# A GRU and an RK4 oscillator in one recurrence: order of the new h, the stage bases and the candidate, and 1 - z scaled by ScalarE

## What is computed

```python
def cell(h, x):                                   # layer 0: GRU
    gi = x @ W_ih + b_ih; gh = h @ W_hh + b_hh
    r = sigmoid(i_r + h_r); z = sigmoid(i_z + h_z)
    n = tanh(i_n + r * h_n)
    return (1.0 - z) * n + z * h
def derivative(q, p, drive):                      # layer 1: four of these per step (RK4)
    dq = q - q**3 / 3.0 - p + drive + tanh(q) @ coupling.T + bias
    dp = EPSILON * (q + ALPHA - BETA * p)
```

## Time and profile before

| | us |
|---|---|
| median of 3 runs (lowest, highest) | 3659.93 (3659.13, 3660.63) |
| the profiled execution, its own time | 3661.45 |
| its span | 3659.7 |
| TensorE busy: matmul, weight load | 3546.2, 3220.4 |
| VectorE, ScalarE, GpSimd busy | 2998.4, 2574.2, 1507.0 |

### The profile page before, as it was taken

The page is one execution under the profiler, slowest core; times in us unless marked ns, Lnnn a source line. Parts: engine busy times, 40 slices in busy tenths (PEclk is TensorE's granted clock), DMA queues, the critical chain, the costliest instruction groups (busy, mean ns, idle before and its releaser), DMA issues.

```text
span 3659.7 us, 298613 instructions
## 1 busy us (share of the span) xinstructions
PE 3546.2 (97%) x115469; PEld 3220.4 (88%) x115469; DVE 2998.4 (82%) x20699; ACT 2574.2 (70%) x22689; POOL 1507.0 (41%) x6169
## 2 busy tenths in 40 slices
PE   8989999999999999999999999999999999999978
PEld 4479999999999999999999999999999999999954
DVE  2078888888888888888888888888888888888876
ACT  3257777777777777777777777777777777777753
POOL 0034444444444444444444444444444444444421
PEclk9999999999999999999999999999999999999978
DMA  3000000000000000000000000000000000000001
GB/s 127 23 25 1 1 1 1 1 1 1 1 1 1 1 1 1 1 1 1 1 1 1 1 1 1 1 1 1 1 1 1 1 1 1 1 1 1 1 2 46
DMA packets 9454, 24.45 MB, mean 7 GB/s; under 512 B 557, under 2 KB 601, under 8 KB 8793
## 3 DMA queue, kind: packets, MB, share of 16 engines
q1 hardware_dynamic: 8832, 19.92, 1.5%
q10 hardware_dynamic: 88, 0.02, 0.0%
HBM read 15.75 MB, written 4.19 MB: 5 GB/s over the span
## 4 chain that ended last, share of the span: by engine, by line
PE 79%; DVE 14%; issue 4%; ACT 3%; DVEq 0%; DMA 0%; ACTq 0%; POOL 0%; POOLq 0%
PE psum L1180 43%; PE psum L1138 29%; PE psum L1108 5%; DVE psum L887 2%; DVE tpart L843 2%; DVE gates L776 2%; ACT tpart L571 1%; PE psum L1283 1%; DVE psum L878 1%; DVE psum L866 1%; DVE fresh L795 1%; DVE narg L787 1%; DVE hs L812 1%; ACT tfull L573 1%; DVE hpart L819 0%
## 5 line engine op out<-in xcount | busy, mean ns | idle before, releaser
L1180 PE MATMUL psum<-tpart,cpl 128*128 128x32 f16 x65536 | 1995.8, 177 | 34.1 <-DVE tpart L843 15.0
L1180 PEld LDWEIGHTS psum<-tpart,cpl 128*128 128x128 f16 x65536 | 1788.7, 96 | 150.9 <-DVE tpart L843 41.5
L1138 PE MATMUL psum<-hpart,whh 128*128 128x32 f16 x49152 | 1622.9, 176 | 28.8 <-DVE hpart L819 24.4
L1138 PEld LDWEIGHTS psum<-hpart,whh 128*128 128x128 f16 x49152 | 1404.1, 96 | 91.5 <-DVE hpart L819 30.4
L843 DVE SCALAR_TENSOR_TENSOR tpart<-tfull,tpart 128x8 f16<-128x8 f32 x4096 | 668.4, 163 | 146.6 <-ACT tfull L573 9.9
L571 ACT ACTIVATE tpart<-psum 128x8 f16<-128x8 f32 x3072 | 544.0, 177 | 245.8 <-DVE psum L887 177.2
L887 DVE TENSOR_REDUCE psum<-psum 128x8 f32<-128x24 f32 x3072 | 585.5, 192 | 133.9 <-PE psum L1180 12.2
L573 ACT ACTIVATE tfull<-psum 128x8 f32<-128x8 f32 x3072 | 529.2, 172 | 0.0
L571 ACT ACTIVATE tpart<-qnext 128x8 f16<-128x8 f32 x1024 | 213.9, 209 | 434.6 <-DVE qnext L887 434.5
L535 ACT ACTIVATE qterm<-psum 128x16 f32<-128x16 f32 x3072 | 400.6, 184 | 111.0 <-DVE psum L866 109.1
L374 POOL TENSOR_TENSOR kept<-rz,hs 128x8 f32<-128x8 f32 x1024 | 209.2, 204 | 466.5 <-ACT rz L500 465.6
(11 more groups left out here) (152 smaller groups left out, 4040.5 us busy)
## 6 DMA issues: line engine op xcount, KB each, us to landing
xrow<-in_x_dram SPq DMA_DIRECT2D x4, 1024.0 KB, 11.3
out_dram<-space SPq DMA_DIRECT2D x16, 256.0 KB, 2.0
wih<-in_L_cond_W_ih_dram SPq DMA_DIRECT2D x3, 1024.0 KB, 9.6
space<-in_L_cond_W_hh_dram SPq DMA_DIRECT2D x1, 3072.0 KB, 18.6
space<-in_L_cond_coupling_dram SPq DMA_DIRECT2D x1, 1024.0 KB, 19.2
xrow<-in_cond_dram SPq DMA_DIRECT2D x1, 1024.0 KB, 4.7
wih<-in_L_cond_Wk_dram SPq DMA_DIRECT2D x1, 1024.0 KB, 5.6
wih<-in_L_cond_Wo_dram SPq DMA_DIRECT2D x1, 1024.0 KB, 8.0
```

Source lines behind the costliest of these rows:

```text
L1138: mm = pe.matmul(gate_out[x][:, :, :, c * B:(c + 1) * B], whh[:, w, k, n * P:(n + 1) * P], copies_in(hpart[:, k, :, :]), start=(c == 0 and ...
L1180: mm = pe.matmul(stage_out[a][:, :, :, col:col + B], cpl[:, w, k, n * P:(n + 1) * P], copies_in(tpart[:, s % 2, k, :, :]), start=(col == 0 ...
```

## The change

VectorE: in stage 2 `base(2)` goes ahead of `sum_gates(1)`; in stage 3 the order becomes `cubic(3)`, `weigh(1)`, `base(3)`, `new_high(1)`, `new_h_full(1)`, `h_low(1)`, and only then `sum_stage(3, 0)` and `sum_stage(3, 1)`. `weigh` multiplies two tensors instead of two tensors and a scalar, since ScalarE now scales `omz` into a new tile `omzs` (`scaled_omz`); the first half's runs behind the terms of stage 0, the second half's between the two halves' tanh of stage 2. `split_tanh` subtracts instead of multiplying by 1.0 and subtracting. ScalarE: in stage 2 the square that feeds `cubic(3)` goes ahead of `candidate(1)`. GpSimd: `keep_part(1)` goes behind the sums of stage 2 instead of stage 1.

```diff
--- before.py
+++ after.py
@@ -116,6 +116,7 @@
         gates = sb("gates", [P, HALVES, HG])
         rz = sb("rz", [P, HALVES, 2 * HC])
         omz = sb("omz", [P, HALVES, HC])
+        omzs = sb("omzs", [P, HALVES, HC])
         gated = sb("gated", [P, HALVES, HC])
         narg = sb("narg", [P, HALVES, HC])
         cand = sb("cand", [P, HALVES, HC])
@@ -255,6 +256,7 @@
 
         h_parts, gibase_ready, ka_read, h_ready = sem_ab("h_parts"), sem("gibase_ready"), sem("ka_read"), sem("h_ready")
         gate_mm, gate_sum, rz_ready, omz_ready = sem_ab("gate_mm"), sem_ab("gate_sum"), sem_ab("rz_ready"), sem_ab("omz_ready")
+        omzs_ready = sem_ab("omzs_ready")
         gated_ready, narg_ready, cand_ready = sem_ab("gated_ready"), sem_ab("narg_ready"), sem_ab("cand_ready")
         kept_ready, fresh_ready, hi_ready, hs_ready = sem_ab("kept_ready"), sem_ab("fresh_ready"), sem_ab("hi_ready"), sem_ab("hs_ready")
 
@@ -406,7 +408,7 @@
                     if s == 1 and tail <= T:
                         next_x1(tail, now)
                         next_uhat(tail)
-                    if s == 1 and gru <= T:
+                    if s == 2 and gru <= T:
                         keep_part(1, gru)
 
                 if tail <= T:
@@ -480,6 +482,8 @@
                 act.reg_load(r, kap[0:1, n:n + 1].bitcast(i32))
             k_unh = act.alloc_register("act_scale_h")
             act.reg_load(k_unh, inv[0:1, 0:1].bitcast(i32))
+            k_h = act.alloc_register("act_scale_up")
+            act.reg_load(k_h, scale[0:1, 2:3].bitcast(i32))
             k_minus = act.alloc_register("act_scale_minus")
             act.reg_load(k_minus, kap[0:1, 5:6].bitcast(i32))
             k_c = act.alloc_register("act_scale_c")
@@ -500,6 +504,11 @@
                 act.activation(rz[:, x, :], gates[:, x, HC:HG], ACT.Sigmoid, scale=k_gate).then_inc(rz_ready[x], 1)
                 act.activation(omz[:, x, :], gates[:, x, 2 * HC:HG], ACT.Sigmoid, scale=k_minus).then_inc(omz_ready[x], 1)
 
+            def scaled_omz(x, v):
+
+                act.wait_ge(omz_ready[x], v)
+                act.activation(omzs[:, x, :], omz[:, x, :], ACT.Copy, scale=k_h).then_inc(omzs_ready[x], 1)
+
             def candidate(x, v):
 
                 act.wait_ge(narg_ready[x], v)
@@ -517,6 +526,8 @@
                 gate_input(v)
                 sigmoids(0, v)
                 sigmoids(1, v)
+                scaled_omz(0, v)
+                scaled_omz(1, v)
                 candidate(0, v)
                 candidate(1, v)
                 plain_h(v)
@@ -574,10 +585,10 @@
                                        scale=k_stage[s]).then_inc(tanh_ready[s][a], 1)
                         if s == 1 and a == 0 and gru <= T:
                             candidate(0, gru)
+                        if s == 2 and a == 0 and gru <= T:
+                            scaled_omz(1, gru)
                     if s == 2:
                         stage_terms(2)
-                        if gru <= T:
-                            candidate(1, gru)
                     arg, s_next = (in_halves(qnext[:, :]), 0) if s == 3 else (qt, s + 1)
                     if s < 3 or tail <= T:
                         act.activation(in_halves(sq[:, s_next, :]), arg, ACT.Square,
@@ -589,6 +600,8 @@
                             sigmoids(0, gru)
                         act.wait_ge(cub_ready, stage_count(1, now))
                         stage_terms(0)
+                        if gru <= T:
+                            scaled_omz(0, gru)
                         if 3 <= tail <= T:
                             plain_h(tail)
                     if s == 1:
@@ -598,6 +611,8 @@
                         stage_terms(1)
                         if gru <= T:
                             sigmoids(1, gru)
+                    if s == 2 and gru <= T:
+                        candidate(1, gru)
                     if s == 2 and gru < T:
                         gate_input(gru + 1)
                     if s == 3 and tail <= T:
@@ -790,10 +805,9 @@
 
             def weigh(x, v):
 
-                dve.wait_ge(omz_ready[x], v)
+                dve.wait_ge(omzs_ready[x], v)
                 dve.wait_ge(cand_ready[x], v)
-                dve.scalar_tensor_tensor(fresh[:, x, :], omz[:, x, :], s_h, cand[:, x, :],
-                                         ALU.mult, ALU.mult).then_inc(fresh_ready[x], 1)
+                dve.tensor_tensor(fresh[:, x, :], omzs[:, x, :], cand[:, x, :], ALU.mult).then_inc(fresh_ready[x], 1)
 
             def new_high(x, v):
 
@@ -840,9 +854,9 @@
             def split_tanh(s, a, v, ready, n):
 
                 dve.wait_ge(ready, n)
-                dve.scalar_tensor_tensor(tpart[:, s % 2, a * HK:(a + 1) * HK, 1, :],
-                                         tfull[:, a * HC:(a + 1) * HC].rearrange("p (k b) -> p k b", b=B), 1.0,
-                                         tpart[:, s % 2, a * HK:(a + 1) * HK, 0, :], ALU.mult, ALU.subtract).then_inc(t_parts[s][a], 1)
+                dve.tensor_tensor(tpart[:, s % 2, a * HK:(a + 1) * HK, 1, :],
+                                  tfull[:, a * HC:(a + 1) * HC].rearrange("p (k b) -> p k b", b=B),
+                                  tpart[:, s % 2, a * HK:(a + 1) * HK, 0, :], ALU.subtract).then_inc(t_parts[s][a], 1)
 
             for a in range(HALVES):
                 split_tanh(0, a, 1, tanh0_ready, a + 1)
@@ -932,8 +946,9 @@
                 if gated_step:
                     new_high(0, gru)
                     new_h_full(0, gru)
+                base(2, now)
+                if gated_step:
                     sum_gates(1, gru)
-                base(2, now)
                 if gru < T:
                     h_low(0, gru)
 
@@ -945,18 +960,17 @@
                     argument(1, gru)
                 split_tanh(3, 0, now, tanh_ready[2][0], now)
                 split_tanh(3, 1, now, tanh_ready[2][1], now)
+                cubic(3, now)
                 if gated_step:
                     weigh(1, gru)
-                cubic(3, now)
+                base(3, now)
                 if gated_step:
                     new_high(1, gru)
-                base(3, now)
-                if gated_step:
                     new_h_full(1, gru)
-
-                sum_stage(3, 0, now)
                 if gru < T:
                     h_low(1, gru)
+
+                sum_stage(3, 0, now)
                 sum_stage(3, 1, now)
                 if tail <= T:
                     split_tanh(0, 0, tail, tanh_ready[3][0], now)
```

## The result

The changed kernel takes 3710.12 us (median of 4 runs, 3707.46 to 3713.26), the kernel before in the same rounds 3660.23. The ratio is 1.0137, 95% interval 1.012 to 1.0155: 49.9 us slower. The forecast was 3731, in a range of 3696 to 3757. The granted clock was 0.989 over the span, as before. Ratios in this document leave out executions in a second, slower state of the chip; e5's slowest run is one.

A forecast was written before the change was run, and what follows sets the result against it. TensorE was nearly always busy, its next stage 0 released by two level chains. A reduce 0.17 later cost 0.16 per step, less 0.02 for the loop turn: 0.14 x 510 = 71 us, median 3731, range 3696 to 3757.

The forecast's parts named there:

- The bound: TensorE's next stage 0 waits for two level releasers, `h_low(1)` and `split_tanh(0, 0)`; shortening only one gains nothing.
- Part 3, the place of the reduce: VectorE, stage 3: the first reduce, now behind `h_low(1)`, starts 0.17 later; stage 0 follows, 0.16 us per step.
- Part 1, the first half: Stage 2, first half of h: `weigh(0)` 0.08 shorter, but `sum_gates(1)` 0.05 later; stage 3 starts 0.04 later.
- Part 2, the candidate: ScalarE, stage 3: `candidate(1)` behind the square comes 0.12 later, 0.05 inherited and 0.07 from the square; `weigh(1)` 6.00, was 5.88.
- Part 1, `scaled_omz`: Two more ScalarE activations fit into free queue time and cost nothing; upper bound 0.10 of delay.
- The turn of the loop: TensorE's loop turn may hide in its new wait, giving back 0 to 0.04 per step; half taken.
- A: Rival, faster: both releasers of stage 0 come earlier, needing `new_high(1)` before 6.07; 0.10 per step, 3609; chance 0.08.
- B: Rival, slower still: `scaled_omz(1)` delays the second tanh pair by 0.10; 0.24 per step, 3782; chance 0.05.
- C: Rival, no change: waits on the own engine cost no queue time, reduce at 6.55; 3660; chance 0.07.
- D: Rival, better cover: loop turn goes wholly, half the stalls fall into new gaps; 0.07 per step, 3696; chance 0.12.
- The rule weighed: Skill's rule that chained semaphores cost nothing extra would make VectorE's order nearly free; rows showed 0.17 of queue time against it.

The follow-up runs named there:

- e5: The kernel before with four steps instead of two in the body of TensorE's loop: 3793.88 us, ratio 1.034 without the slowest run.
- e1: The changed kernel with `h_low(1)` back between the two reduces of stage 3: 3604.47 us, 0.9847 of the kernel before.
- e2: The kernel before with only `h_low(1)` moved ahead of `sum_stage(3, 0)`: 3762.54 us, ratio 1.0279.
- e4: The changed kernel with the scale back in VectorE's `weigh` and both `scaled_omz` activations dropped: 3770.62 us, 1.0303 of the kernel before.
- e3: The changed kernel with ScalarE's `candidate(1)` ahead of the square again: 3736.28 us, 1.0212 of the kernel before.
- e7: The changed kernel with the scale back in VectorE's `weigh`, both `scaled_omz` activations kept but unread: 3769.41 us, 1.0299 of the kernel before.
- e13: The changed kernel with one step instead of two in the body of TensorE's loop: 3710.38 us, 1.0135 of the kernel before.

## Why the prediction was right, and where its sizes were off

**The bound.** Two releasers of stage 0 were level, and only one of them got better. Right: `h_low(1)` came 0.11 earlier, the split 0.13 later, and the step followed the split.

**Part 3, the place of the reduce.** The step that decided the case, right in mechanism: 0.27 (forecast 0.26) from `new_h_full(1)` to `h_low(1)`, 0.11 on to the reduce. e1 and e2 show it from both sides.

**Part 1, the first half.** Off in size, and in sign: `split_tanh(3, 0)` was to be 0.05 later and was 0.06 earlier. Two rows of before did not carry over. `new_high(0)` with 0.20, and `new_h_full(0)` 0.13 behind it, became 0.17 and 0.08, so the gate sum was 0.01 later and not 0.05. `argument(1)` went from 0.27 to 0.23 and the split from 0.20 behind it to 0.14. Nothing in these instructions was changed. e4 shows the slow write again (0.21, and 0.14 to the next) as soon as `weigh(0)` is longer, e3 in the second half. What changed is what GpSimd does beside them: its `next_uhat` (L352, now L354) beside `new_high(0)`, its sum (L404, now L406) beside `argument(1)`. GpSimd in the step before and in the one after:

```profile
1804.29 0.22 POOL L352 TENSOR_TENSOR uhat<-uscaled,bhat 128x16 f32<-128x16 f32 x1 [0.55 <-ACT uscaled L552]
1805.23 0.25 POOL L404 TENSOR_TENSOR sums<-sums,qterm 128x32 f32<-128x32 f32 x1
```

```profile
1814.88 0.22 POOL L354 TENSOR_TENSOR uhat<-uscaled,bhat 128x16 f32<-128x16 f32 x1 [0.55 <-ACT uscaled L563]
1815.28 0.25 POOL L406 TENSOR_TENSOR sums<-sums,qterm 128x32 f32<-128x32 f32 x1 [0.18 <-ACT qterm L546]
```

`next_uhat` starts 0.03 ahead of the slow `new_high(0)` (1804.32) and 0.04 behind the fast one (1814.84). Over the traces of all these kernels but e5's, `new_high` was slow (0.19 or more) in each of the 2407 cases in which `next_uhat` started 0.01 to 0.06 ahead of it, and in none of the 3832 in which it started as much behind. GpSimd's sum starts together with the slow `argument(1)` (1805.23); now that `keep_part(1)` stands behind that sum, it starts 0.54 ahead of it, and in the changed kernel no `argument` takes 0.25 or more, against 453 before. In e3 it is `phat` (L419) that runs beside `new_high(1)`: it ended 0.20 or 0.21 behind the start of all 485 writes that took 0.19 or more there, and 0.23 or 0.24 behind in the 479 fast cases of the changed kernel. So part 1 left out GpSimd, which runs beside these instructions. That this overlap is the cause is read from the traces; no run tried it by itself.

**Part 2, the candidate.** Forecast 0.12 later: measured 0.05. Of the 0.07 too much, the part that part 1 had passed on was wrong; the pitch from square to candidate was 0.06 (forecast 0.07). `weigh(1)` measured 0.06 later instead of 0.12. `weigh(1)` itself took 0.17, not the 0.15 that was taken from `new_h_full`, which made `new_high(1)` 0.02 later than its sum had it. In sum the reduce was 0.13 later, not 0.17, and the step 0.13, not 0.16: a mean step of 6.56, not 6.60. The wait for `h_parts[1]` was to be mostly gone (a block of 0.67 to 0.70); the block took 0.77, so only 0.06 of the 0.16 went. That the swap is no loss at all once `cubic(3)` stands in front (e3) the prediction did not see, since it costed the swap against the old order.

**Part 1, `scaled_omz`.** Booked at nothing, bounded by 0.10 a step. e4 against e7: nothing. In the trace the second tanh pair starts 0.19 behind the activation (1815.75 to 1815.94), as its reduce lets it.

**The turn of the loop.** The term with the bounds 0 and 0.04, taken at 0.02. It is wholly given back: e13 shows it. That is another 10 us.

**The sum.** 0.13 for the step, less 0.04 for the turn, gives 0.09; the mean step grew by 0.094, so by difference the stalls without a releaser cost about what they did. That makes 48 of the 49.9 us. The forecast of 0.14 was too large by the 0.03 of parts 1 and 2 and the 0.02 of the turn: 0.05 x 510 = 25 us, of which 21 were seen.

**The rivals.** A failed where it was said to: `new_high(1)` did not start before 5.22, with 5.08 needed for it (6.07 on the prediction's clock). B is excluded by e7 against e4, C by e1 and e2. D was half right: the turn did go wholly, the stalls were not hidden.

**The rule weighed.** By the Trainium skill, "VectorE: DVE Perf Modes", section "The DRAIN you can't avoid", a semaphore between chained instructions costs nothing extra. Here a chained pair keeps 0.27 (`new_h_full(1)` to `h_low(1)`) and an unchained one 0.08 (`new_high(1)` to `new_h_full(1)`), and 106 us hang on it in e1. For chains of instructions of this size the measurement decides against taking the order in the queue as free. It does not separate the semaphore from the dependence itself: no run here chains two such instructions without the semaphore.

## What to carry to other kernels

Before an instruction is moved ahead in an in-order queue, look at what it waits for: if that is the result of the instruction right in front of it, the move turns a gap that another instruction was filling into idle time, and that other one pays, here 106 us in 512 steps, 0.21 us in each. Where two releasers are level, look at which of them the edit makes late; the wait that it visibly shortens may not be the one that counts. And take a change apart before it is discarded: all of this one but one move was worth 56 us (e1), and that move cost 106.

## What the runs showed of the hardware that was not expected

- A loop body of four steps on TensorE (1792 matmuls and weight loads) is, by the rows of e5, fetched anew while it runs: 326 packets and 5.34 MB on its instruction queue and waits of up to 5.2 us, against 17 packets and 0.28 MB with two steps.
- A turn of TensorE's loop costs 0.12 us when the engine has work ready (29 us for 255 turns), and nothing in front of a wait of 0.29 us.
- An unchanged VectorE instruction, fp16 into `hpart`, takes 0.17 or 0.21 us, and the one behind it follows at 0.08 or 0.14. With GpSimd's `next_uhat` starting 0.01 to 0.06 us ahead of it, it was slow in 2407 of 2407 cases, with `next_uhat` as much behind in 0 of 3832.
